# Seven products instead of eight for part of the first stage of an eight-core RWKV + FFN kernel

## What is computed

```
xn  = layernorm(x)
k   = xn @ Wk.T;  r = xn @ Wr.T                 # 1024 x 1024 each
y   = wkv_scan(w, u, k, r)                      # recurrence over the tokens, per channel
att = (sigmoid(r) * y) @ Wo.T
g   = xn @ w_gate.T / 127;  up = xn @ w_up.T / 127   # 3072 x 1024 each, int32 weights
ffn = (silu(g) * up) @ w_down.T / 127
out = x + att + ffn
```

## Time and profile before

| | us |
|---|---|
| median of 3 runs | 1299.21 (1297.23 to 1324.13) |
| the profiled execution | 1298.55 |
| its span, slowest core | 1297.0 (the eight cores: 1294.2 to 1297.0) |
| TensorE busy in the span | 1280.1 (99%) |
| VectorE busy | 913.8 (70%) |
| ScalarE busy | 511.2 (39%) |

### The profile page before, as it was taken

How to read it: one execution, slowest core, us unless ns; L and a number is a source line. 1 busy time by engine, 2 the same in 40 slices (tenths; PEclk the granted TensorE clock), 3 DMA queues, 4 the chain that set the end, 5 groups by cost and what they waited for, 6 DMA issues and landing times.

```text
span 1297.0 us, 18789 instructions; the slowest of 8 cores (1294.2 to 1297.0 us)
## 1 busy us (share of the span) xinstructions
PE 1280.1 (99%) x6064; PEld 586.9 (45%) x6064; DVE 913.8 (70%) x1473; ACT 511.2 (39%) x874; POOL 98.4 (8%) x190
## 2 busy tenths in 40 slices
PE   6999999999999999999999999999999999999999
PEld 4444444444444444444444444444444444444444
DVE  5666666625897777787888777688788877767721
ACT  5555455422325444432333444433242444442200
POOL 0111112000000000000000000000000000000000
PEclk9999999999999999999999999999999999999999
DMA  8566746996645445576555544568466554444121
GB/s 195 80 121 122 134 81 102 165 215 132 126 98 114 82 82 98 133 159 148 107 121 114 98 83 81 98 155 186 99 126 111 105 98 88 81 76 98 50 81 57
DMA packets 75407, 145.93 MB, mean 113 GB/s; under 512 B 31152, under 2 KB 34224, under 8 KB 75184
## 3 DMA queue, kind: packets, MB, share of 16 engines
q0 software_dynamic: 26640, 88.09, 39.1%
q1 hardware_dynamic: 23328, 50.35, 13.7%
q10 hardware_dynamic: 25344, 6.29, 3.1%
HBM read 209.72 MB, written 16.78 MB: 175 GB/s over the span
## 4 chain that ended last, share of the span: by engine, by line
PE 90%; DVE 4%; DVEq 2%; DMA 2%; issue 1%; ACT 0%; SPq 0%; ACTq 0%
PE ps L358 28%; PE ps_o L436 22%; PE ps L348 14%; PE ps L352 13%; PE ps_o L443 7%; PE ps_o L358 5%; DMA wd_bf<-x_tm 2%; DVE work L678 1%; DVEq L685 1%; DVEq L673 1%; DVE work L686 1%; DVEq L691 0%; DVE work L676 0%; DVE x_all L718 0%; DVE x_all L714 0%
## 5 line engine op out<-in xcount | busy, mean ns | idle before, releaser
L436 PE MATMUL ps_o<-wd_bf,h_act 128*128 128x512 bf16 x1536 | 342.0, 379 | 0.0
L436 PEld LDWEIGHTS ps_o<-wd_bf,h_act 128*128 128x128 bf16 x1536 | 150.3, 98 | 181.2
L348 PE MATMUL ps<-xn,ring 128*128 128x512 f16 x896 | 211.6, 379 | 2.7 <-DMA ring<-w_gu 2.5
L352 PE MATMUL ps<-xn,ring 128*128 128x512 f16 x896 | 211.7, 379 | 0.0
L549 ACT COPY work<-ps 128x512 f32<-128x512 f32 x216 | 126.3, 586 | 177.9 <-PE ps L358 172.0
L523 ACT ACTIVATE work<-work 128x512 f32<-128x512 f32 x64 | 40.3, 630 | 263.5 <-DVE work L692 263.3
L348 PEld LDWEIGHTS ps<-xn,ring 128*128 128x128 bf16 (+1 forms) x896 | 87.4, 98 | 108.0 <-issue 3.1
L352 PEld LDWEIGHTS ps<-xn,ring 128*128 128x128 bf16 (+1 forms) x896 | 87.7, 98 | 105.7
L358 PE MATMUL ps<-x_all,work 128*128 128x512 f16 x576 | 130.7, 379 | 1.5 <-ACT work L549 1.5
L443 PE MATMUL ps_o<-wo_bf,outp 128*128 128x512 bf16 x512 | 121.0, 379 | 0.0
L746 DVE TENSOR_TENSOR work<-work,ps 128x512 f32<-128x512 f32 x144 | 98.4, 684 | 16.4 <-ACT work L549 16.3
(11 more groups left out here) (79 smaller groups left out, 1266.0 us busy)
## 6 DMA issues: line engine op xcount, KB each, us to landing
ring<-w_gu POOLq DMA_DIRECT2D x72, 512.0 KB, 7.7
ring<-w_kr POOLq DMA_DIRECT2D x56, 512.0 KB, 7.4
xres<-x_tm SPq DMA_DIRECT2D x64, 256.0 KB, 4.9
out_tm<-xres SPq DMA_DIRECT2D x64, 256.0 KB, 3.0
x_all<-x_tm SPq DMA_DIRECT2D x28, 512.0 KB, 9.1
outp<-w_gu POOLq DMA_DIRECT2D x24, 512.0 KB, 7.8
wd_bf<-w_dn POOLq DMA_DIRECT2D x24, 128.0 KB, 8.6
wd_bf<-w_dn POOLq DMA_DIRECT2D x4, 768.0 KB, 24.0
```

The source lines that it names most:

```text
L348: ins = te.matmul(bank(kind, idx, 0), w[:, gc * D:(gc + 1) * D], xn[c % 2][:, gc, :], start=(gc == 0), stop=(gc == G - 1))
L352: ins = te.matmul(bank(kind, idx, 1), w[:, C + gc * D:C + (gc + 1) * D], xn[c % 2][:, gc, :], start=(gc == 0), stop=(gc == G - 1))
L436: te.matmul(ps_o[i % 2], h_act[c % 2][:, hg * TC + tt * D:hg * TC + (tt + 1) * D], wd_bf[:, half, hg * 512:(hg + 1) * 512], start=(hg == 0 ...
```

## The change

1. **Seven quads in the first stage** (`Q0 = G - 1`). Rows 0, 1, 2 and 5, 8, 11, ... 23 of chunks 0 and 1 stay gu units (20 of them), rows (3,4), (6,7), ... (21,22) go into seven quads, one per step. After the opening (gu units 0 to 2 of chunk 0, one k/r unit, gu units 3 to 5 of chunk 1), the stage has seven steps of one quad, one k/r unit of chunk 0 and two gu units.
2. **The k/r units of chunk 1 move** out of the first stage into output stage c = 0, one ahead of each output unit, as it is in the stages behind; their weight rows are loaded again for them.
3. **The quad's scratch** in the first stage lies in the second half of w_down's buffer (`wide[0]` in wd_bf[:, 1]), because `work` is in use by the k/r units. So `wd_second` and `wo_second` now wait for the last quad, and stand in the queue behind four ring rows of chunk 1.
4. **The ring** has six buffers in the first stage (the two halves of outp[1] count), and the x tiles 8 to 11 are loaded in stage c = 0, after the last quad.
5. **The opening**: transposes of tiles 4 to 7 go to ps_o and wait for its evacuation only, tile 7's stands between the halves of the first k/r unit, and layernorm of tile 7 stands later on VectorE and ScalarE, behind `gate(1)`.
6. **The last output unit** is done in two halves of 256 columns (`out_last`), each with an addition and a store of its own; the second half goes to ps0.

```diff
-for s0 in range(1, 2 * G):
-    SLOTS += [("gu", 3 * s0), ("gu", 3 * s0 + 1), ("gu", 3 * s0 + 2), ("kr", s0)]
+SLOTS = [("tr", l0) for l0 in range(NT)] + [("gu", 0), ("gu", 1), ("gu", 2), ("kr", 0)]
+SLOTS += [("gu", 3), ("gu", 4), ("gu", 5)]
...
+def quad_at(p, k):
+    return k if p == 0 else Q0 + QP * (p - 1) + k
+def quad_rows(p, k):
+    return (3 * k + 3, 3 * k + 4) if p == 0 else (2 * k, 2 * k + 1)
...
+        wide = [wd_bf[:, 1, :].bitcast(F32), work]
...
# gpsimd
-                    if n == NS:
+                    if n == NS + R:
                         gp.wait_ge(sem["s_xt"], 2 * NX)
+                        gp.wait_ge(sem["v_hq"], 4 * Q0)
                         for k in range(4):
                             wd_second(k)
                         wo_second()
...
# tensor, acquire()
+                    if kind == "gu" and idx >= 6:
+                        if idx % 2:
+                            te.wait_ge(sem["v_cc"], CPQ * (idx // 2 - 2))
+                        else:
+                            te.wait_ge(sem["s_sq"], 4 * (idx // 2 - 3) + 3)
+                            te.wait_ge(sem["v_hq"], 4 * (idx // 2 - 3) + 3)
+                        return
# tensor, quad(p, k)
+                    if p == 0 and k == 0:
+                        te.wait_ge(sem["v_h"], 4)
+                    elif p == 0:
+                        te.wait_ge(sem["v_zA"], k + 1)
...
                     te.wait_ge(sem["v_s"], 4 * qd + 1)
+                    if p == 0:
+                        te.wait_ge(sem["v_h"], 5 if k == 0 else 6 + 2 * k)
# tensor, the first stage
-                for s in range(1, 2 * G):
-                    for i in range(3 * s, 3 * s + 3):
-                        proj("gu", i, GU[i][0], "t_g", "t_u")
-                    proj("kr", s, KR[s][0], "t_k", "t_r")
+                for i in range(3, 6):
+                    proj("gu", i, 1, "t_g", "t_u")
+                for s in range(1, G):
+                    quad(0, s - 1)
+                    proj("kr", s, 0, "t_k", "t_r")
+                    for i in range(4 + 2 * s, 6 + 2 * s):
+                        proj("gu", i, GU[i][0], "t_g", "t_u")
# tensor, out_last(i): new
+                    for m in range(2):
+                        dst = ps_o[i % 2][:, 0:256] if m == 0 else pair[0][0][:, 0:256]
+                        for hg in range(HG):
+                            te.matmul(dst, h_act[c % 2][...],
+                                      wd_bf[:, half, hg * 512 + 256 * m:hg * 512 + 256 * (m + 1)],
+                                      start=(hg == 0), stop=False)
...
# scalar, quad(p, k): the reciprocal of the last k/r unit inside it
                     copied(u3b[w][1], bank_x(k, 1), 9)
+                    if p == 0:
+                        att_rec(k)
                     sc.wait_ge(sem["v_cc"], CPQ * qd + 1)
# scalar, the first stage
-                for s in range(1, 2 * G):
-                    for i in range(3 * s, 3 * s + 3):
-                        gate(i)
-                    att_rec(s - 1)
-                    att_exp(s)
+                for s in range(1, G):
+                    quad(0, s - 1)
+                    att_exp(s)
+                    for i in range(4 + 2 * s, 6 + 2 * s):
+                        gate(i)
# vector, the first stage
-                for s in range(1, 2 * G):
-                    att_scan(s - 1)
-                    ffn_h(3 * s)
-                    att_den(s - 1)
-                    ffn_h(3 * s + 1)
-                    ffn_h(3 * s + 2)
-                    att_max(s)
-                    att_out(s - 1)
+                for s in range(1, G):
+                    quad(0, s - 1)
+                    if s + 1 < G:
+                        w_sums(0, s)
+                    att_max(s)
+                    ffn_h(4 + 2 * s)
+                    att_scan(s)
+                    ffn_h(5 + 2 * s)
+                    att_den(s)
```

More of the change, by code:

```diff
@@ L45 @@
-SLOT_AT = {u: q for q, u in enumerate(SLOTS)}
[L47 to L59, removed]
+for s0 in range(1, G):
+    GU += [(0, 3 * s0 + 2), (1, 3 * s0 + 2)]
+NG = len(GU)
+KR = [(c0, g0) for c0 in range(NCH) for g0 in range(G)]
@@ L60, with ring_row @@
+RING_AT[("kr", 0)] = 3
+def ring_row(kind, row, c, uses, end):
+    for u in uses:
+        RING_AT[u] = len(RING)
+    RING.append((kind, row, c))
+    RING_END.append(end)
+for s0 in range(1, G):
+    for r0 in range(2):
+        ring_row("q", quad_rows(0, s0 - 1)[r0], 0, [("q", s0 - 1, r0)], PPQ * s0)
+    ring_row("kr", s0, 0, [("kr", s0)], s0 + 1)
+    ring_row("gu", 3 * s0 + 2, 0, [("gu", 4 + 2 * s0), ("gu", 5 + 2 * s0)], 6 + 2 * s0)
 NS = len(RING)
-for c0 in range(2, NCH):
+for c0 in range(1, NCH):
@@ L76 @@
     if n0 < NS:
-        s0 = n0 % R
+        s0 = n0 % (R + 2)
     elif kind0 == "kr":
-        s0 = row0 % R
+        s0 = (row0 + 2) % R if c0 == 1 else row0 % R
     else:
@@ L260, in _ @@
                                 x_load(NT * (c + 3) + g - 2)
-                out_store(8 * NCH - 1)
+                last = 8 * NCH - 1
+                t0, c0 = out_rows(last)
+                for m, done in enumerate([("v_half", 1), ("v_add", last + 1)]):
+                    sy.wait_ge(sem[done[0]], done[1])
+                    sy.dma_start(out=out_hbm[t0:t0 + D, c0 + 256 * m:c0 + 256 * (m + 1)],
+                                 in_=xres[last % NXR][:, 256 * m:256 * (m + 1)]).then_inc(sem[f"st{last % NXR}"], 16)
                 for i in range(NXR):
-                    sy.wait_ge(sem[f"st{i}"], 16 * len(range(i, 8 * NCH, NXR)))
+                    sy.wait_ge(sem[f"st{i}"], 16 * (len(range(i, 8 * NCH, NXR)) + (i == last % NXR)))
             @blk.gpsimd
@@ L737, in w_sums, with quad @@
                     ve.tensor_sub(s4, a[:, :, 1, :], s2).then_inc(sem["v_s"], 1)
-                def quad(qd):
-                    k = qd % QP
+                def quad(p, k):
+                    qd = quad_at(p, k)
+                    rows = quad_rows(p, k)
+                    w = min(p, 1)
                     def h_tile(row, ch):
-                        return h_act[ch][:, (2 * k + row) * TC:(2 * k + row + 1) * TC]
+                        return h_act[ch][:, rows[row] * TC:(rows[row] + 1) * TC]
                     def summed(buf, src):
```

274 lines of the change are left out of this document (161 added, 113 removed).

## The result

The changed kernel took 1351.16 us (median of 4 executions, 1343.8 to 1531.56) beside 1299.03 of the kernel before on the same chip: ratio 1.0387, 95% interval 1.0332 to 1.0443. It is slower by 3.9%, where 1.9% was forecast and 1337 was the end of the range; the quickest execution, 1343.8, lies beyond it too. The profiled execution took 1350.19 us. In the execution of 1531.56 the mean granted clock was 0.84 to 0.93, and such executions are left out of every ratio and interval here.

A forecast was written before the change was run, and what follows sets the result against it. TensorE, busy 99%, was taken as bound by its count of matmuls. Matmuls -12.1, opening -3.7, end -0.4, new waits +40.0, stage c = 0 +1 make +24.8 us: 1324 us, 1.9% slower, range 1304 to 1337.

The forecast's parts named there:

- The loop's mechanism and size: First-stage steps: turns of ScalarE and VectorE close a loop of 28.5 us against TensorE's 22.44, six rounds costing 36.8 us.
- six waits on zA: Sign of being right: TensorE waits six times, 4 to 5 us each, at the quads' first product for VectorE's zA.
- The third product's wait of 1.4 us: In each step, TensorE waits about 1.4 us at the quad's third product for the V pair.
- The clock falls in the waits: Rival: after new waits in the steps the clock drops to 1.2 GHz, 3 to 20 us in all, 1327 to 1344; chance 0.08.
- the single gap of the opening: Ground for a steady clock: in a gap of 4 us with TensorE nearly idle, the granted clock stayed at 1.00.
- bounds 0 and 8 us; I take 1: Stage c = 0: late weight row and ScalarE behind blocked transposes cost 0 to 8 us, 1 taken in the sum.
- The opening: 3.7 forecast: Opening: the wait of 3.76 us for tile 5's transpose goes away, gain 3.7 us, bounds 1 and 4.
- The end: Last output unit: addition and store of 256 columns instead of 512 gain 0.4 us together, bounds 0 and 1.
- the matmuls: First stage: seven quads replace 28 gu units, 56 matmuls fewer at 0.2158 us each, gain 12.1 us.
- the 16 us that the prediction counted: Whole kernel: gains of matmuls, opening and end together, 16.2 us, set against about 41 us of TensorE's waits.
- the stall in c = 0: Rival: late weight row or ScalarE behind transposes in stage c = 0 adds 6 to 15 us, 1330 to 1339; chance 0.13.
- slower by over 2%: Whole kernel: outcome above 1325.2 us, given a chance of 0.45.

The follow-up runs named there:

- e3: Changed kernel with 64 unused 128x128 matmuls at the end of each of the first six steps, where TensorE waits: 1340.2 us, ratio 1.0316 to the kernel before.
- e1: Changed kernel with a k/r unit's reciprocal and its result moved out of the quad to the end of the step: 1314.47 us, ratio 1.0116.
- e2: Changed kernel with the k/r unit's maximum put ahead of the next quad's four sums of weights on VectorE: 1325.54 us, ratio 1.0234.
- e5: Changed kernel with the two scans put ahead of the product of each step's first gu unit on VectorE: 1325.93 us, ratio 1.0199.
- e9: Changed kernel with layernorm, transposes and x loads of chunk 2 in stage c = 0 one output unit later: 1338.16 and 1338.5 us, ratio 1.0306.
- e6: Changed kernel with reciprocal and result moved to the step's end and the scans ahead of the step's first gu product: 1303.02 us, ratio 1.0017.
- e7: Changed kernel with reciprocal, result and scans moved, and chunk 2's layernorm, transposes and x loads in stage c = 0 two output units later: 1288.92 us, ratio 0.9911.
- e8: Changed kernel with only chunk 2's layernorm, transposes and x loads in stage c = 0 two output units later, steps untouched: 1345.61 us, ratio 1.0353.

## Why the prediction was wrong, step by step

- **The loop's mechanism and size were right.** Four table loads in a step, six waits on zA, and the loop as worked out: 28.5 us against 28.76 where the clock held (e3), and the three links that were cut or moved (e1, e2, e5) gave steps of 24.2, 26.2 and 26.5 us. TensorE at 99% before had hidden two engines that had no turn to spare in this order. The third product's wait of 1.4 us is not in the trace of after, since the half pace ahead of it fills it; with the clock held it shows as 1.2.
- **"The clock falls in the waits", chance 0.08, was the case.** The step that failed here is that the sum holds the clock at 1.00 in the new waits, on the ground of the single gap of the opening. Its price lies in the steps: 216.9 us from the opening to the first output unit (e9) against 211.8 (e3), 5 us, near the low end of the 3 to 20 given. The profiled execution lost 3 more by its stretch at 0.81 (220.0 against 216.9); the quickest execution of the kernel after took 1343.8.
- **Stage c = 0: "bounds 0 and 8 us; I take 1"** was the mis-sized term: the stage took 7.4 us more than forecast, so 8.4 for the 1. I had followed the first transpose only. It was issued some 27 us into the stage of core 1 (22 forecast) and held ScalarE 1.70 us; it was the second one, 11 us later, that was blocked for 12.5, and the sixth output unit then stood. e9 shows it: one unit later, and the stage is at 79.6. That this is not the half pace's doing is shown by e6, whose steps have no wait and whose stage c = 0 is as slow.
- **Nothing was set down for what comes behind.** The row "L400 <- DVE work L811" is the first quad of c = 2, which waits for sums of weights. VectorE's k/r units follow each other there at 10.45 us (409.86 to 420.31 on core 1), TensorE's at 10.36: a lag that stage c = 0 leaves is not made up in c = 1 (read from these paces; no run tests it alone). It cost 2.6 to 4.1 us by core, and the half pace behind it some 1.6 more (on cores 0 and 1 16 matmuls in 5.24 and 5.33 us for 3.61; core 5 alone shows no fall): 5 us in all. One unit of shift leaves that wait (3.0 to 4.2 us in e9), two take it away (0.4 in e7).
- **The opening: 3.7 forecast, 0.8 found,** and that is not clear of chance: the kernels with the same new opening end it at 38.4 to 40.0 us in the mean of their cores. The term was read on the slowest core alone. That core was the slowest because it had that wait.
- **The end** (0.6 for 0.4) and the matmuls are as forecast: with neither waits nor lag (e7) the kernel gains 0.9%, 11 of the 16 us that the prediction counted, the opening making most of the difference.
- **The chances.** I held the clock, the stall in c = 0 and the loop for cases of which one comes true. They don't exclude each other, and all came true together: e3 has the loop and the stall with the clock held in the steps, e9 the loop and the clock without the stall. (The chances for slower by over 2% add up to 0.46, not 0.45.) Added up by the prediction's own numbers they reach 1324 + 6 + 3 = 1333 at the least and 1324 + 15 + 20 = 1359 at the most, which holds what was measured.

## What to carry to other kernels

When an engine at 99% is relieved, walk the order of the engines behind it once round, with durations of the trace: here that gave the new pace to 1%, and cutting two links of it (the reciprocal, the scans) turned +3.9% into +0.2% (e6). Then price what a new wait brings with it, the pace after it and the lag that the next stage can't make up, and add these to the main case instead of setting them beside it. Where a transfer is moved into a stage, list what else its queues are asked for there: with the transposes one unit later instead of two the kernel took 1338.3 us instead of 1345.6 (e9, e8). And read a gain on all cores before counting on it.

## What the runs showed of the hardware

- After steady work at full clock, waits of 4.1 to 4.4 us ahead of a quad were followed by half pace in all 126 cases, those of 3.3 to 3.5 in 30 of 48, waits up to 1.7 us in none of 144. From the restart it lasts 2.6 to 6.0 us, 4.4 in the mean, and costs about 0.9 us a step (216.9 - 211.8 over six), less than the 1.7 us that the first eight matmuls lose (3.57 for 1.89), because part of it lies in waits that were there anyway. The Trainium skill (TensorE: Matmul & The Clock Gate, "Why this matters for your kernels") warns of gaps between bursts, and the waits of 4.1 to 4.4 us here agree.
- A switch of ScalarE's table costs its 1.28 us and no more: in the kernel after, the load at 103.05 is followed by its silu at 104.35, and VectorE has it at 105.12. The drain of some 1.38 us that the Trainium skill adds (ScalarE: Activation LUTs, "What ACT_TABLE_LOAD costs") is not seen: by an estimate from that figure, 28.5 + 4 x 1.38, the steps of e3 would be some 34 us instead of 28.76.
- The second DMA transpose issued while GpSimd's queue still moved the second halves held ScalarE for 8.9 to 14.8 us on the cores of the kernel before, 12.5 to 16.8 in the kernel after and up to 19.68 in e6 (core 1, at 242.65); the first took 1.4 to 1.9 in the kernels before and after. One issued 0.3 us behind three weight rows landed after 21.3 us (e8) where 4.7 is that kernel's median.
- A granted clock of 0.81 over 160 us on six of eight cores was seen in one of the twelve profiled executions, on no core of the others. The kernel after's execution of 1352.14 us may have had it on two cores (not shown by any trace): their mean clocks are 0.966 and 0.968, those of the other six 0.981 to 0.986. Nothing here tells what brought it on.
